# Softplus sums of a selective scan on GpSimd, its rounding on ScalarE, and the first chunk's gates projected behind its first step sizes

## Chip, cores and metric

One core of one Trainium2 chip runs the whole kernel. The metric is the device time of one execution in microseconds (us), as the median of several runs. The engines are TensorE (PE, matrix products into PSUM), VectorE (DVE), ScalarE (ACT, activation functions), GpSimd (POOL, SBUF only) and SyncE (SP, which only issues DMAs here). Each works through its own queue in order; they meet at semaphores.

## What is computed

A decoder layer over 2048 tokens of 256 features: a Mamba block with a feed-forward net, a cross attention over 1601 tokens, and a soft mixture of experts. The change touches the Mamba block alone:

```python
def mamba_block(x, ...):
    xz = x @ in_proj_w.T
    u, z = jnp.split(xz, 2, axis=-1)
    u = jax.nn.silu(causal_dwconv(u, conv_w, conv_b))
    x_dbl = u @ x_proj_w.T
    dt = x_dbl[..., :DT_RANK]
    ...
    delta = jax.nn.softplus(dt @ dt_proj_w.T + dt_proj_b)
    A = -jnp.exp(A_log)
    y = selective_scan(u, delta, A, Bm, Cm) + u * D
    y = y * jax.nn.silu(z)
    return y @ out_proj_w.T
```

The scan runs over time for each of 512 channels and 16 states: `h = exp(delta*A)*h + (delta*u)*B`, and `y` is the sum of `h*C` over the states.

## The kernel before

The tokens are cut into four chunks (`c`) of 512. In a chunk the 512 channels stand as four blocks of 128 partitions; two blocks are a half (`p` = 0 or 1), which is why most of the operands here are 128x1024. A chunk has 32 slots (`i`, `NU`), one for each half and state: slots 0 to 15 scan the first half, 16 to 31 the second. Over all chunks a slot is numbered `w` (0 to 127).

In a slot, ACT makes the decays `exp(delta*A)` of both blocks into PSUM (`decays`, L567), POOL makes `delta*u*B` for both (`scan_input`, L431, into a ring of three), DVE scans each block (L864), multiplies by C (`times_c`, L875) and keeps the last column (L882), and PE adds the products up in PSUM with a unit matrix (`add_states`, L1317). For one pair of slots in four POOL adds the two first (`add_pair`, L437), and PE waits for that. POOL may start the input of slot w when the scans of slot w-3 are done; ACT the decays of slot w when the products of slot w-2 are. B and C come by DMA on SP's queue, each two states ahead.

All else is laid by hand between these, by the number of the slot: each engine has one loop over chunks and slots with `if i == ...`. ACT's loop stands one slot ahead: at `i` it first makes the decays of slot i+1. Besides the scan of chunk c the loops carry the input side of chunk c+1 (transposing, in-projection, convolution `convolution` L812 and L816 at slots 9 to 12, gates `gate_input` L529, x_proj, step sizes) and the output side of chunk c-1 (`first_norm`, hidden blocks with Gelu at slots 23 to 30, `ffn_out`; `second_residual` L911, `second_norm` L921 and `mamba_out` L926 come in slots 2, 6 and 7 of the chunk after that).

The softplus is written as `relu(x) + log(1+e) + (e - ((1+e) - 1))` with `e = exp(-|x|)`. ACT makes |x| and relu (`step_input`, L544, L545), e (`step_exp`, L550) and the logarithm (`step_log`, L555); DVE the rounding `(1+e)-1` in one instruction of two operations (`step_rounded`, L826), the rest `e - ...` (`step_rest`, L831), the sum with the logarithm (`step_sum`, L837), and the addition to the relu (`step_size`, L844). `step_channels` (L852) is `delta*u`. Each is one instruction over a half, and happens eight times: for the first half of chunk 0 before the loop, for the second half of each chunk at slots 6 to 9, and for the first half of the next chunk at slots 24 to 28:

```python
if i == 6:
    step_rounded(c, 1)
...
if i == 8:
    step_sum(c, 1)
    step_size(c, 1)
if i == 9:
    step_channels(c, 1)
```

Before the loop, the first chunk is brought to its first step sizes: in-projection of the channels, then of the gates, convolution, Silus, x_proj (L1285), step sizes.

## Time and profile before

| | |
|---|---|
| median of 3 runs | 1638.02 us (1636.45 to 1638.27) |
| profiled execution, first to last instruction | 1636.5 us |
| scan of the Mamba block (first and last scan) | 49.7 to 660.7 us |
| busy over the span: PE, DVE, ACT, POOL | 1336.6, 797.4, 904.6, 402.9 us |
| busy from 100 to 200 us: PE, DVE, ACT, POOL | 63.4, 99.3, 48.4, 61.5 us |
| granted TensorE clock, mean | 0.90; 0.71 from 50 to 100 us, 0.78 from 100 to 200 us |

The profile was made on one execution; the times stand for that one. The page of the profile says of the granted TensorE clock what share of 2.4 GHz it is: 1.0 or 0.5 (1.2 GHz) at any moment. A float32 product shows as several passes of one instruction; "x8" in a row is their count. In the timeline, neighbouring instructions of one line are merged into one row, and a bracket names the idle time of the engine before it and what ended it.

### The profile page before, as it was taken

The numbers are of one execution on the slowest core, as the hardware profiler recorded it, in microseconds if no ns is written. First come the engines' busy times: TensorE is split into PE (matmuls) and PEld (weight loads), VectorE is DVE, ScalarE is ACT, GpSimd is POOL, SyncE is SP. The second block draws the span as 40 slices with busy tenths as digits, with TensorE's granted clock in tenths as the row PEclk, the third lists the DMA queues.
The fourth block names the chain that finished last, engine by engine and source line by source line (L and its number), as shares of the span: only waits on it lengthen the run. The fifth ranks groups of instructions, "written<-read, shape, count | busy, mean of one in ns | idle before, by whom it ended". The sixth has DMA issues, their size and how long they took to land.

```text
span 1636.5 us, 15496 instructions
## 1 busy us (share of the span) xinstructions
PE 1336.6 (82%) x5511; PEld 628.7 (38%) x5511; DVE 797.4 (49%) x1213; ACT 904.6 (55%) x1164; POOL 402.9 (25%) x177
## 2 busy tenths in 40 slices
PE   6477566887598748896735999999999988979999
PEld 2122123343334324653521223223223234568887
DVE  3899989989998899216520002001011016461011
ACT  3536444654466436122435997998998944751310
POOL 0637655654455466015030000000000001000000
PEclk9588787999789878998756999999999988989999
DMA  5323332332243233102994000000000000011701
GB/s 184 118 78 129 129 115 86 122 116 77 82 138 116 77 128 116 45 8 49 102 112 39 1 1 1 1 1 0 0 0 0 0 0 1 1 52 35 325 14 39
DMA packets 35633, 107.96 MB, mean 66 GB/s; under 512 B 3650, under 2 KB 14146, under 8 KB 32915
## 3 DMA queue, kind: packets, MB, share of 16 engines
q1 hardware_dynamic: 35572, 107.19, 23.7%
q8 instruction: 34, 0.56, 0.1%
q14 instruction: 27, 0.22, 0.1%
HBM read 93.60 MB, written 2.36 MB: 59 GB/s over the span
## 4 chain that ended last, share of the span: by engine, by line
PE 47%; DVE 24%; ACT 13%; issue 8%; DMA 5%; SPq 1%; POOL 1%; DVEq 0%; ACTq 0%; POOLq 0%
DVE ps L864 13%; PE ps L1558 10%; PE ps L1543 9%; ACT arena L706 6%; PE ps L1362 4%; PE ps L1667 4%; DMA arena<-arena 4%; PE ps L1708 3%; PE ps L1317 3%; DVE arena L875 2%; PE ps L1685 2%; PE ps L1696 2%; PE ps L1248 2%; SPq L377 1%; PE ps L1588 1%
## 5 line engine op out<-in xcount | busy, mean ns | idle before, releaser
L706 ACT ACTIVATE arena<-ps,bound 128x1024 f32<-128x1024 f32 (+1 forms) x416 | 421.1, 1215 | 26.7 <-PE ps L1543 26.7
L431 POOL TENSOR_TENSOR arena<-arena 128x1024 f32<-128x1024 f32 x128 | 300.7, 2353 | 262.0 <-DVE ps L864 218.1
L864 DVE TENSOR_TENSOR_SCAN ps<-ps,arena 128x512 f32<-128x512 f32 x256 | 327.3, 1279 | 18.1 <-ACT ps L567 13.7
L1317 PE MATMUL ps<-arena,ident 128*128 128x512 f32 x452 | 245.1, 683 | 106.1 <-POOL arena L437 66.1
L567 ACT ACTIVATE ps<-arena 128x512 f32<-128x512 f32 x256 | 173.1, 689 | 269.1 <-DVE arena L882 175.5
L1543 PE MATMUL ps<-arena 97*128 (+3 forms) x832 | 218.9, 385 | 22.8 <-issue 20.7
L1558 PE MATMUL ps<-arena 128*32 128x512 f32 (+1 forms) x1664 | 222.8, 607 | 1.1 <-ACT arena L706 0.9
L1317 PEld LDWEIGHTS ps<-arena,ident 128*128 128x128 f32 x452 | 91.5, 214 | 243.3 <-issue 89.0
L1141 DVE COPY arena<-ps 128x512 f32<-128x512 f32 x16 | 11.1, 691 | 355.8 <-PE ps L1558 355.8
L419 POOL TENSOR_TENSOR rstd<-ve,mhalf 128x4 f32<-128x4 f32 (+3 forms) x18 | 23.5, 1308 | 625.0 <-DVE ve L1166 469.9
L875 DVE TENSOR_TENSOR arena<-ps,arena 128x512 f32<-128x512 f32 x256 | 171.4, 669 | 0.0
L1543 PEld LDWEIGHTS ps<-arena 97*128 97x128 bf16 (+1 forms) x832 | 67.5, 99 | 227.0 <-ACT arena L706 140.6
L1248 PE MATMUL ps<-ident,arena 128*128 128x128 f32 x392 | 58.7, 291 | 40.4 <-DVE arena L1051 13.7
L1248 PEld LDWEIGHTS ps<-ident,arena 128*128 128x128 f32 x392 | 45.1, 147 | 76.0 <-issue 57.5
L1362 PE MATMUL ps<-arena 128*128 128x256 f32 x256 | 62.5, 400 | 12.1 <-ACT arena L583 12.1
L1558 PEld LDWEIGHTS ps<-arena 128*32 128x32 f32 (+1 forms) x1664 | 32.9, 108 | 95.5 <-ACT arena L706 78.3
L1262 PE MATMUL ps<-arena 128*128 128x512 f32 x128 | 62.9, 639 | 4.1 <-DVE arena L895 2.4
L1353 PE MATMUL ps<-arena 128*128 128x512 f32 x128 | 59.9, 615 | 5.5 <-ACT arena L583 4.8
L1667 PE MATMUL ps<-arena 128*128 128x257 f32 x256 | 58.6, 393 | 2.5 <-ACT arena L752 2.5
L1362 PEld LDWEIGHTS ps<-arena 128*128 128x128 f32 x256 | 50.0, 199 | 26.8 <-ACT arena L583 15.4
L1632 PE MATMUL ps<-arena 128*128 128x512 f32 x128 | 59.6, 609 | 0.0
L1708 PE MATMUL ps<-arena 128*128 128x256 f32 x256 | 55.5, 379 | 0.0
(178 smaller groups left out, 1386.5 us busy)
## 6 DMA issues: line engine op xcount, KB each, us to landing
arena<-bc_scratch SPq DMA_DIRECT2D x128, 512.0 KB, 3.7
arena<-in_mw SPq DMA_DIRECT2D x16, 1024.0 KB, 8.7
arena<-arena SPq DMA_DIRECT2D x48, 128.0 KB, 14.8
arena<-arena SPq DMA_DIRECT2D x12, 400.2 KB, 16.4
arena<-in_w SPq DMA_DIRECT2D x2, 1024.0 KB
out<-xt SPq DMA_DIRECT2D x4, 512.0 KB, 2.9
xt<-in_x SPq DMA_DIRECT2D x1, 1536.0 KB
arena<-in_ctx SPq DMA_DIRECT2D x1, 1200.8 KB, 7.8
```

The lines of the kernel that those rows point to most:

```text
L431: pool.tensor_tensor(dbu[:, w % DR], du[:, DP * p:DP * p + DP], over(bg[:, w // BG % 2, n % BG], DP), ALU.mult).then_inc(S["dbu_ready"], 1)
L567: act.activation(decay_bank(w, x), delta[:, d], ACT.Exp, scale=neg_a[:, d, n:n + 1]).then_inc(S["da_ready"], 1)
L706: act.activation(flat(prob[0:n, v % 2, 2 * h:2 * h + 2]), ps[0:n, 2 * (r % 3):2 * (r % 3) + 2, :].rearrange("p a b -> p (a b)"), ACT.Exp, ...
L864: dve.tensor_tensor_scan(decay_bank(w, x), decay_bank(w, x), dbu[:, w % DR, x], carry[:, d, n:n + 1], ALU.mult, ALU.add).then_inc(S["scan_ ...
L875: dve.tensor_tensor(state(w)[:, x], decay_bank(w, x), cg[:, w // BG % 2, n % BG], ALU.mult).then_inc(S["hc_ready"], 1)
L1248: return pe.transpose(dst, src, ident[:, :])
L1317: last = mm(bank(x), ident[:, :], state(2 * j + s)[:, x], start=False, stop=(j % HP == HP - 1 and (j in SUMMED or s == 1)))
L1362: mm(acc, gate[:, f, tok(i)], w2[:, f], start=(f == 0), stop=False)
L1543: last = mm(ps[0:n, 2 * (r % 3) + x, :], kx[0:XR + 1, head, b * P:b * P + n], qx[0:XR + 1, head, c * C:c * C + C] if first else qx[0:XR + ...
L1558: last = mm(ps[2 * HD * x:2 * HD * x + 2 * HD, 6 + g % 2, :], vx[0:n, b, G * g + x, :], prob[0:n, v % 2, x], start=(b == 0), stop=(b == KB ...
L1667: last = mm(ps[:, 4 + x if x < 4 else x - 4, 0:DM + 1], lg[:, t, tok(x)], xn[:, t, :], start=(t == 0), stop=(t == TT - 1))
L1708: last = mm(ps[:, t % 8, 0:DM], cwt[:, x, tok(t)], eo[:, x], start=(x == 0), stop=(x == NE - 1))
```

## The change

1. `step_rounded` is gone. ACT makes `1+e` and then `(1+e)-1` with two Identity activations in `step_log`, the logarithm after them.
2. `step_rest`, `step_sum` and `step_size` go to POOL's queue: for the second half behind the inputs of slots 7, 9 and 11, for the first half of the next chunk behind those of 24, 25 and 26. Only the first half of chunk 0 stays on DVE.
3. `step_channels` stays on DVE, at slot 14 instead of 9, and at slot 29 instead of 28.
4. In the first chunk, gates are projected behind x_proj and the first step sizes; ACT takes their Silus in its slot 1.

```diff
@@ -448,11 +448,42 @@
...
+            def step_rest(c, p):
+                h = c * DP + p
+                pool.wait_ge(S["sp_act"], h * 6 + 5)
+                pool.tensor_tensor(flat(sp_cor), flat(sp_exp), flat(sp_cor), ALU.subtract).then_inc(S["sp_step"], 1)
+
+            def step_sum(c, p):
+                h = c * DP + p
+                pool.wait_ge(S["sp_act"], h * 6 + 6)
+                pool.wait_ge(S["sp_step"], h * 2 + 1)
+                pool.tensor_tensor(flat(sp_cor), flat(sp_cor), flat(sp_ln), ALU.add).then_inc(S["sp_step"], 1)
+
+            def step_size(c, p):
+                h = c * DP + p
+                half = flat(delta[:, DP * p:DP * p + DP])
+                pool.wait_ge(S["sp_in"], h * DP + DP)
+                pool.wait_ge(S["sp_step"], h * 2 + 2)
+                pool.tensor_tensor(half, half, flat(sp_cor), ALU.add).then_inc(S["delta_ready"], 1)
+
             layer_norm_root(0)
             for c in range(NC):
+                more = c + 1 < NC
                 for i in range(NU):
                     w = c * NU + i
                     scan_input(w)
+                    if i == 7:
+                        step_rest(c, 1)
+                    if i == 9:
+                        step_sum(c, 1)
+                    if i == 11:
+                        step_size(c, 1)
+                    if i == 24 and more:
+                        step_rest(c + 1, 0)
+                    if i == 25 and more:
+                        step_sum(c + 1, 0)
+                    if i == 26 and more:
+                        step_size(c + 1, 0)
                     if w % 2 == 0 and w // 2 - 2 in SUMMED:
                         add_pair(w // 2 - 2)
...
 
             def step_exp(c, p):
                 h = c * DP + p
-                act.wait_ge(S["sp_act"], h * 4 + 2)
+                act.wait_ge(S["sp_act"], h * 6 + 2)
                 act.activation(flat(sp_exp), flat(sp_exp), ACT.Exp, scale=-1.0).then_inc(S["sp_act"], 1)
 
             def step_log(c, p):
                 h = c * DP + p
-                act.wait_ge(S["sp_act"], h * 4 + 3)
-                act.activation(flat(sp_ln), flat(sp_exp), ACT.Ln, bias=1.0).then_inc(S["sp_act"], 1)
+                act.wait_ge(S["sp_act"], h * 6 + 3)
+                act.activation(flat(sp_ln), flat(sp_exp), ACT.Identity, bias=1.0).then_inc(S["sp_act"], 1)
+                act.wait_ge(S["sp_act"], h * 6 + 4)
+                act.activation(flat(sp_cor), flat(sp_ln), ACT.Identity, bias=-1.0).then_inc(S["sp_act"], 1)
+                act.activation(flat(sp_ln), flat(sp_ln), ACT.Ln).then_inc(S["sp_act"], 1)
...
             for d in range(DB):
                 conv_input(0, d)
             for d in range(DB):
-                gate_input(0, d)
-            for d in range(DB):
                 channel(0, d)
             rank_b_c(0)
             step_input(0, 0)
@@ -606,6 +638,9 @@
                 for i in range(NU):
                     if c * NU + i + 1 < NW_ALL:
                         decays(c * NU + i + 1)
+                    if i == 1 and c == 0:
+                        for d in range(DB):
+                            gate_input(0, d)
                     if i == 3 and c >= 2:
                         second_squares(c - 2)
...
-            def step_rounded(c, p):
-                h = c * DP + p
-                dve.wait_ge(S["sp_act"], h * 4 + 3)
-                dve.tensor_scalar(flat(sp_cor), flat(sp_exp), 1.0, 1.0, ALU.add, ALU.subtract).then_inc(S["sp_step"], 1)
-
...
-                if i == 6:
-                    step_rounded(c, 1)
-                    if c >= 2:
-                        second_norm(c - 2)
-                if i == 7:
-                    step_rest(c, 1)
-                    if c >= 2:
-                        mamba_out(c - 2)
-                if i == 8:
-                    step_sum(c, 1)
-                    step_size(c, 1)
-                if i == 9:
+                if i == 6 and c >= 2:
+                    second_norm(c - 2)
+                if i == 7 and c >= 2:
+                    mamba_out(c - 2)
+                if i == 14:
                     step_channels(c, 1)
                 if i in (9, 10, 11, 12) and more:
                     convolution(c + 1, i - 9)
...
-                if more:
-                    if i == 24:
-                        step_rounded(c + 1, 0)
-                    if i == 25:
-                        step_rest(c + 1, 0)
-                    if i == 26:
-                        step_sum(c + 1, 0)
-                    if i == 27:
-                        step_size(c + 1, 0)
-                    if i == 28:
-                        step_channels(c + 1, 0)
+                if i == 29 and more:
+                    step_channels(c + 1, 0)
...
             conv_keep(0)
-            step_rounded(0, 0)
             step_rest(0, 0)
             step_sum(0, 0)
             step_size(0, 0)
...
             def gates(c, d):
                 if d < 2:
-                    pe.wait_ge(S["u_raw"], c * DB + DP + d + 1)
+                    if c:
+                        pe.wait_ge(S["u_raw"], c * DB + DP + d + 1)
+                    else:
+                        pe.wait_ge(S["sp_in"], d + 1)
                     if c >= 2:
                         pe.wait_ge(S["hsum_ready"], (c - 2) * 2 + d + 1)
                 else:
...
             pe.wait_ge(S["w_first"], 16 * 3)
             for d in range(DB):
                 channels(0, d)
+            rank_b_c(0)
+            step_input(0, 0)
             for d in range(DB):
                 gates(0, d)
-            rank_b_c(0)
-            step_input(0, 0)
             pe.wait_ge(S["w_mamba"], 16 * 6)
             pe.wait_ge(S["prep_dve"], 1 + DB)
```

**POOL's queue in chunk 0, from the input of slot 7 on.** L431 is `scan_input`, L437 `add_pair`; before:

```order
L431 TENSOR_TENSOR arena<-arena 128x1024 [waits scan_done]
L431 TENSOR_TENSOR arena<-arena 128x1024 [waits scan_done,b_even]
L437 TENSOR_TENSOR arena<-arena 128x1024 [waits hc_ready]
L431 TENSOR_TENSOR arena<-arena 128x1024 [waits scan_done]
L431 TENSOR_TENSOR arena<-arena 128x1024 [waits scan_done,b_odd]
L431 TENSOR_TENSOR arena<-arena 128x1024 [waits scan_done]
L431 TENSOR_TENSOR arena<-arena 128x1024 [waits scan_done,b_even]
```

and after, where L454 is `step_rest`, L460 `step_sum` and L467 `step_size`:

```order
L431 TENSOR_TENSOR arena<-arena 128x1024 [waits scan_done]
L454 TENSOR_TENSOR arena<-arena 128x1024 [waits sp_act]
L431 TENSOR_TENSOR arena<-arena 128x1024 [waits scan_done,b_even]
L437 TENSOR_TENSOR arena<-arena 128x1024 [waits hc_ready]
L431 TENSOR_TENSOR arena<-arena 128x1024 [waits scan_done]
L460 TENSOR_TENSOR arena<-arena 128x1024 [waits sp_step,sp_act]
L431 TENSOR_TENSOR arena<-arena 128x1024 [waits scan_done,b_odd]
L431 TENSOR_TENSOR arena<-arena 128x1024 [waits scan_done]
L467 TENSOR_TENSOR arena<-arena 128x1024 [waits sp_step,sp_in]
L431 TENSOR_TENSOR arena<-arena 128x1024 [waits scan_done,b_even]
```

Each of the three stands behind one input and ahead of the next; the pair of states (L437) is behind the rest.

**POOL's queue in chunk 0, from the input of slot 24 on**, before:

```order
L431 TENSOR_TENSOR arena<-arena 128x1024 [waits scan_done,b_even]
L437 TENSOR_TENSOR arena<-arena 128x1024 [waits hc_ready]
L431 TENSOR_TENSOR arena<-arena 128x1024 [waits scan_done]
L431 TENSOR_TENSOR arena<-arena 128x1024 [waits scan_done,b_odd]
L431 TENSOR_TENSOR arena<-arena 128x1024 [waits scan_done]
```

and after (the same lines):

```order
L431 TENSOR_TENSOR arena<-arena 128x1024 [waits scan_done,b_even]
L454 TENSOR_TENSOR arena<-arena 128x1024 [waits sp_act]
L437 TENSOR_TENSOR arena<-arena 128x1024 [waits hc_ready]
L431 TENSOR_TENSOR arena<-arena 128x1024 [waits scan_done]
L460 TENSOR_TENSOR arena<-arena 128x1024 [waits sp_step,sp_act]
L431 TENSOR_TENSOR arena<-arena 128x1024 [waits scan_done,b_odd]
L467 TENSOR_TENSOR arena<-arena 128x1024 [waits sp_step,sp_in]
L431 TENSOR_TENSOR arena<-arena 128x1024 [waits scan_done]
```

The rest, which waits for ACT, now stands between the input of slot 24 and the pair; sum and addition follow behind the next two inputs.

**ACT's queue ahead of the loop.** L517 copies the channels, L529 are the gates' Silus, L522 the channels' Silus, L535 the copy of x_proj's result; before:

```order
L517 ACTIVATE arena<-ps 128x512 [waits u_ps] x4
L529 ACT_TABLE_LOAD
L529 ACTIVATE arena<-ps 128x512 [waits z_ps] x4
L522 ACTIVATE arena<-arena 128x512 [waits conv_step] x4
L535 ACTIVATE arena<-ps 48x512 [waits xdbl_ps]
```

and after, where L548 is the copy, L553 the channels' Silus, L566 the copy of x_proj and L575 and L576 are |x| and relu:

```order
L548 ACTIVATE arena<-ps 128x512 [waits u_ps] x4
L553 ACT_TABLE_LOAD
L553 ACTIVATE arena<-arena 128x512 [waits conv_step] x4
L566 ACTIVATE arena<-ps 48x512 [waits xdbl_ps]
L575 ACTIVATE arena<-ps,chan 128x512 [waits dt_ps]
```

The gates' Silus no longer stand there.

**ACT's queue from the first exponential (L550) into slot 1.** Before (L555 is the logarithm, L567 the decays):

```order
L550 ACTIVATE arena<-arena 128x1024 [waits sp_act]
L555 ACT_TABLE_LOAD
L555 ACTIVATE arena<-arena 128x1024 [waits sp_act]
L567 ACT_TABLE_LOAD
L567 ACTIVATE ps<-arena 128x512 [waits delta_ready]
L567 ACTIVATE ps<-arena 128x512 x3
L567 ACTIVATE ps<-arena 128x512 [waits carry_done,hc_ready]
L567 ACTIVATE ps<-arena 128x512 [waits hc_ready]
L567 ACTIVATE ps<-arena 128x512 [waits carry_done,hc_ready]
L567 ACTIVATE ps<-arena 128x512 [waits hc_ready]
```

and after (L586 and L588 Identity, L589 the logarithm, L601 the decays, L560 the gates' Silus):

```order
L586 ACTIVATE arena<-arena 128x1024 [waits sp_act]
L588 ACTIVATE arena<-arena 128x1024 [waits sp_act]
L589 ACT_TABLE_LOAD
L589 ACTIVATE arena<-arena 128x1024
L601 ACT_TABLE_LOAD
L601 ACTIVATE ps<-arena 128x512 [waits delta_ready]
L601 ACTIVATE ps<-arena 128x512 x3
L601 ACTIVATE ps<-arena 128x512 [waits carry_done,hc_ready]
L601 ACTIVATE ps<-arena 128x512 [waits hc_ready]
L560 ACT_TABLE_LOAD
L560 ACTIVATE arena<-ps 128x512 [waits z_ps] x4
L601 ACT_TABLE_LOAD [waits carry_done]
```

Two Identity activations stand ahead of the logarithm's table, and the four Silus with their table, and one more for the decays, between the decays of slots 2 and 3.

## Rows read from the trace of the kernel before

**Rows 1.** Waits of DVE, 40 to 700 us: who <- whom: total us, times, longest.

```profile
DVE arena L911 <- PE ps L1364: 38.2, 5, 11.3
```

**Rows 2.** Groups by line, DVE and POOL, 0 to 900 us (columns as the page's part 5).

```profile
L864 DVE TENSOR_TENSOR_SCAN ps<-ps,arena 128x512 f32<-128x512 f32 x256 | 327.3, 1279 | 18.1 <-ACT ps L567 13.7 <-POOL arena L431 4.1
...
L831 DVE TENSOR_TENSOR arena<-arena 128x1024 f32<-128x1024 f32 x8 | 10.4, 1294 | 0.0
...
L837 DVE TENSOR_TENSOR arena<-arena 128x1024 f32<-128x1024 f32 x8 | 9.8, 1225 | 0.4 <-ACT arena L555 0.4
L844 DVE TENSOR_TENSOR arena<-arena 128x1024 f32<-128x1024 f32 x8 | 9.8, 1219 | 0.5
...
L826 DVE TENSOR_SCALAR arena<-arena 128x1024 f32<-128x1024 f32 x8 | 5.5, 693 | 12.0 <-ACT arena L550 12.0
...
L431 POOL TENSOR_TENSOR arena<-arena 128x1024 f32<-128x1024 f32 x128 | 300.7, 2353 | 262.0 <-DVE ps L864 218.1 <-DVE arena L852 37.8 <-DMA arena<-bc_scratch 6.0
```

**Rows 3.** Timeline, 0 to 75 us (start us, us, engine line op out<-in xcount [idle before]).

```profile
26.48 2.33 DVE L816 SCALAR_TENSOR_TENSOR arena<-arena,chan 128x512 f32<-128x512 f32 x3
...
30.00 2.17 ACT L522 ACTIVATE arena<-arena 128x512 f32<-128x512 f32 x4
...
34.41 0.59 ACT L535 ACTIVATE arena<-ps 48x512 f32<-48x512 f32 x1 [2.23 <-PE ps L1285]
```

**Rows 4.** Timeline, the same window, slots 1 to 3 of the first chunk.

```profile
54.65 0.69 ACT L567 ACTIVATE ps<-arena 128x512 f32<-128x512 f32 x1 [1.03 <-DVE arena L875]
...
61.60 3.78 PE L1300 MATMUL ps<-arena 16*128 16x512 f32 x4
...
63.48 1.29 DVE L864 TENSOR_TENSOR_SCAN ps<-ps,arena 128x512 f32<-128x512 f32 x1 [1.60 <-POOL arena L431]
```

**Rows 5.** Timeline, chunk 0, slots 23 to 28: DVE and ACT.

```profile
160.64 1.28 DVE L864 TENSOR_TENSOR_SCAN ps<-ps,arena 128x512 f32<-128x512 f32 x1
...
163.16 1.04 ACT L550 ACTIVATE arena<-arena 128x1024 f32<-128x1024 f32 x1
...
164.22 1.28 ACT L555 ACT_TABLE_LOAD   x1
...
164.26 1.28 DVE L864 TENSOR_TENSOR_SCAN ps<-ps,arena 128x512 f32<-128x512 f32 x1
...
165.52 1.06 ACT L555 ACTIVATE arena<-arena 128x1024 f32<-128x1024 f32 x1
...
166.04 0.71 DVE L826 TENSOR_SCALAR arena<-arena 128x1024 f32<-128x1024 f32 x1
...
184.77 1.22 DVE L852 TENSOR_TENSOR arena<-arena 128x1024 f32<-128x1024 f32 x1
```

**Rows 6.** Timeline, chunk 1, slots 23 to 30: PE, ACT and DVE.

```profile
313.35 1.98 PE L1317 MATMUL ps<-arena,ident 128*128 128x512 f32 x4 [1.85 <-POOL arena L437]
315.17 3.60 PE L1353 MATMUL ps<-arena 128*128 128x512 f32 x8
...
315.15 1.04 ACT L550 ACTIVATE arena<-arena 128x1024 f32<-128x1024 f32 x1
...
337.19 1.23 DVE L852 TENSOR_TENSOR arena<-arena 128x1024 f32<-128x1024 f32 x1
...
349.03 5.41 PE L1362 MATMUL ps<-arena 128*128 128x256 f32 x16 [5.28 <-ACT arena L583]
```

**Rows 7.** Timeline, chunk 1, slots 6 and 7: ACT and DVE.

```profile
224.31 1.06 ACT L550 ACTIVATE arena<-arena 128x1024 f32<-128x1024 f32 x1
...
229.88 1.29 DVE L864 TENSOR_TENSOR_SCAN ps<-ps,arena 128x512 f32<-128x512 f32 x1 [1.64 <-ACT ps L567]
```

**Rows 8.** Timeline, chunk 2, slot 6: DVE and POOL.

```profile
388.33 0.68 DVE L826 TENSOR_SCALAR arena<-arena 128x1024 f32<-128x1024 f32 x1
...
388.49 2.72 POOL L437 TENSOR_TENSOR arena<-arena 128x1024 f32<-128x1024 f32 x1 [1.66 <-DVE arena L875]
388.93 3.76 DVE L921 SCALAR_TENSOR_TENSOR arena<-arena,rstd,scales 128x256 f32<-128x256 f32 x4
```

More of the change, by code:

```diff
@@ L834, in step_sum @@
                 h = c * DP + p
-                dve.wait_ge(S["sp_act"], h * 4 + 4)
-                dve.wait_ge(S["sp_step"], h * 3 + 2)
+                dve.wait_ge(S["sp_act"], h * 6 + 6)
+                dve.wait_ge(S["sp_step"], h * 2 + 1)
                 dve.tensor_tensor(flat(sp_cor), flat(sp_cor), flat(sp_ln), ALU.add).then_inc(S["sp_step"], 1)
@@ L1281, in rank_b_c @@
             def rank_b_c(c):
-                pe.wait_ge(S["z_ready"], c * DB + 3)
+                if c:
+                    pe.wait_ge(S["z_ready"], c * DB + 3)
                 for d in range(DB):
@@ L1291, in step_input @@
                     pe.wait_ge(S["xdbl_ready"], c + 1)
-                    pe.wait_ge(S["z_ready"], c * DB + DB)
+                    if c:
+                        pe.wait_ge(S["z_ready"], c * DB + DB)
                     if c >= 2:
@@ L1296, in step_input @@
                     pe.wait_ge(S["sp_in"], c * DB + DP)
+                    if c == 0:
+                        pe.wait_ge(S["z_ready"], DB)
                     if c >= 2:
```

4 lines of the change are left out of this document (2 added, 2 removed).

## Prediction

> **What bounds the kernel now.** I read the waits of VectorE (DVE) first. Between 40 and 700 us, the stretch of the Mamba scan, its residual adds wait 38.2 us for TensorE (PE) [rows 1], and its scans 13.7 us for ScalarE (ACT) and 4.1 for GpSimd (POOL) [rows 2]; nearly everything else is DVE at work. So DVE sets the pace of the scan, one slot after another: a slot without extra work is 3.62 us long (160.64 to 164.26), and what follows the first scan and multiply of a slot starts 1.78 us behind the slot [rows 5]. An instruction taken from DVE is then worth its duration, as long as POOL has the next scan's input, and ACT its decays, in time. The question is whether they still have. The second view is therefore the timeline around the places where a half of the step sizes is made: seven times inside the loop, four times at slots 5 to 9 (the second half of a chunk) and three times at slots 23 to 28 (the first half of the next).
>
> **What leaves DVE.** Seven times a rounding (0.69), a rest (1.29), a sum (1.23) and an addition (1.22) [rows 2]: 4.43 each, 31 us in all. POOL pays 2.35 us for an instruction of the same shape [rows 2], so it gets 7 x 7.05 = 49 us. ACT gets two Identity passes in the place of the rounding; they aren't in the trace, and I take the 1.05 us of its exponential over the same 128x1024 elements [rows 5]; they cost more than nothing and there is no reason for more than 1.3. Seven times 2.1 is 15 us. Both engines have the room on average. What counts is the order on POOL's queue.
>
> **The first half of the next chunk, three times.** POOL runs ahead of DVE: it makes the input of slot w once scan w-3 is over. Behind the input of slot 24 it now meets the rest, which waits for ACT, and everything queued behind it waits too: the pair of states (the same shape, so 2.35) and the input of slot 25. In chunk 0 the exponential ends at 164.20 [rows 5]. Two Identity passes: 166.3. Rest, pair and input, 3 x 2.35: 173.35, and only then can scan 25 start (it could at 167.9). Then sum and input 26: 178.05, addition and input 27: 182.75; a slot lasts 3.62, so POOL sets both. Slot 28 starts at 182.75 + 3.62 = 186.4. Before it was 184.77 - 1.78 = 183.0 [rows 5]. So this place loses **3.4 us** where it should win 4.4.
>
> In chunk 1 the pair matters as well: PE stands before it (PE waits 1.85 us for it at 313.35, [rows 6]) with the feed-forward's matmuls behind it, and ACT's Gelu waits for those in front of the decays of slot 26. Exponential done 316.19 [rows 6], Identity 318.3, rest 320.65, pair 323.0 (before: 313.3). PE has been idle for over 10 us then; four passes at the lower clock take 3.8 us [rows 4], so 326.8; the eight passes of the first two hidden blocks take 3.6 at the full clock [rows 6], about 4 here: 330.8. Gelu 0.7 (as a decay of the same shape), table 1.28, decay 0.69 [rows 4, 5]: slot 26 starts at 333.5, slot 28 at 340.7. Before: 337.19 - 1.78 = 335.4 [rows 6]. **5.3 us** lost; if PE does not come into it, POOL's chain alone gives 338.4, or 3.0. Chunk 2 has the same order of work and a table of times that is within 0.4 us of this: 5.0. The three places: **+13.7 us** (9.4 to 14).
>
> **The second half, four times, without collisions.** Here ACT is one slot earlier against POOL, and the rest's wait does no harm. But ACT is on the path: in chunk 1 scan 7 waits 1.64 us for the decays that stand behind exponential, table, logarithm, table [rows 7]. With 2.1 more it starts at about 231.9 instead of 229.88. The three sums of 3.74 are gone behind it: -1.7. In chunk 0 the same shift, and sums that took 4.3 (one was held up): -2.3. In chunks 2 and 3 a norm (L921, 3.76 us) stands in the same slot and hides the shift: -3.7 each. Together **-11.4**.
>
> **The collisions.** Where the two engines read SBUF at once the trace shows that one holds the other up. POOL's pair wants to start at 388.49, while the rounding runs (388.33 to 389.01): it takes 2.72 instead of 2.35. The next DVE instruction, the norm's first, asks at 388.93, and is done only when POOL has finished at 391.2: four instructions that need under 2 take 3.76 [rows 8]. So POOL gets its turn between two DVE instructions, and DVE then waits for POOL's whole instruction. The scans and multiplies, whose states lie in PSUM, are not held up (256 scans, mean 1.28 [rows 2]). The Trainium skill's page "GPSIMD Engine Reference", section "Key points", names contention with DVE instructions of two SBUF inputs or in a two-port mode; by that rule, which speaks against this change, the trace agrees.
>
> Before, POOL's one input per slot ran beside PSUM work, and the convolution of the next chunk (slots 9 to 12; the last three of its four instructions take 2.33 us [rows 3], all SBUF) met an idle POOL. Now POOL is behind. Chunk 1: the exponential ends at 225.37 [rows 7], the rest starts at 227.5, and then follow without a gap input 8, pair, input 9, sum, input 10 (to 241.6), input 11, addition (to 246.3). DVE reaches the convolution at 231.9 + 2 x 3.62 + 1.78 = 240.9. The rest of input 10, all of input 11 and the addition go in between its four instructions: 0.7 + 2.35 + 2.35 = 5.4 us. Chunk 0 comes out the same (5.3), chunk 2 at 4.5; chunk 3 has no convolution. In chunks 2 and 3 the final addition of slot 7 waits 0.8 for the pair. Together **+17.0**. The bounds are nothing and this sum: between them the row with the turn taken decides.
>
> **The start.** The gates' Silus stood in front of those of the convolution. The convolution ends at 28.81, the first Silu started only at 30.00 and x_proj was read at 34.41 [rows 3]. Now the last Silu runs at once: 28.9 + 0.6 + two passes 0.9 = 30.4, a gain of 4.0 (1.8 if PE has fallen to the lower clock meanwhile). The logarithm is needed 2.1 later behind it: -1.9. In slot 1 ACT then has four Silus and two more tables: from 55.34 - 1.9 [rows 4] table 1.28 and two Silus 1.2, then PE's two blocks of four passes, 1.9 to 3.8 each [rows 4], Silu 0.6, table 1.28, decay 0.69: scan 3 between 63.6 and 65.5, against 63.48 [rows 4], where POOL's input made it wait 1.60. So the whole start comes to 0 to +2, or up to +4 with the low clock; **+1.0**. A rule on the two table loads: on the trace the load starts 0.02 us behind the exponential and the logarithm 0.02 behind the load [rows 5], 1.28 in all. The Trainium skill ("ScalarE: Activation LUTs", section "What ACT_TABLE_LOAD costs") puts a switch at some 2.66 us with its drain; by it the start would be 2.8 worse, as an estimate. I go by the row.
>
> **Sum.** 13.7 - 11.4 + 17.0 + 1.0 = +20.3 us. The profiled execution's span is 1636.5 us, inside the three runs (1636.45 to 1638.27); I add it to their median: 1638.0 + 20.3 = **1658.3 us**. Nothing behind the scan changes. PE's waits ahead of the residual adds don't swallow it: that chain starts from the last Gelu (PE waits 5.28 us for it at 349.03, [rows 6]), and this moves with the slots.
>
> **Rivals.**
> 1. DVE keeps the interface through a chain of its own instructions and waits once only, for the POOL instruction under way: about 5 us of the 17. +8.3, 1646.3. Against it: 388.93 [rows 8].
> 2. There are no collisions: +3.3, 1641.3. Against it the same row.
> 3. The cover holds, and the kernel is **faster**: POOL delivers the sums without making a scan wait. At slot 24 this needs the rest to start by 167.88 - 7.05 = 160.8; the exponential alone ends at 164.20 [rows 5]. Were it so, three times -4.4, with -11.4 and +1.0: -23.6, 1614.4. It could come about only if ACT reached the step's exponential some 5.5 us earlier against DVE; nothing in the change moves it.
> 4. The residual adds' waits on PE (38.2 us in all [rows 1]) do absorb what chunks 1 and 2 lose at slots 24 to 28: 10.3 less, 1648; with no collisions as well, -7.0 and 1631.0. Against it: the 5.28 us.
>
> The new order of the queues shows the sums on POOL in the places said, so that the change does what it says is not in doubt.
>
> **Chances.** A measurement of this kernel tells about 0.2% (3.3 us) from no change. Forecast 0.62 (its own range 1650 to 1667: the bounds of the second, third and last term). Rival 1: 0.16. Rival 2: 0.09, about half of it within 0.2%. Rival 3: 0.04. Rival 4: 0.09, with 0.02 on the fast side. So slower 0.86, same 0.08, faster 0.06. The range that should hold it 8 times in 10 takes in rival 1 and most of rival 4: 1643 to 1667.
>
> **What would show it.** Right: POOL waits for ACT once in slot 24 of chunks 0 to 2, and DVE's scans wait for POOL's input some 7 us at each such place, 20 us in all where it was 4.1; the convolution's instructions show single durations of 2.5 to 3 us; ACT shows two tables more. Wrong: convolution instructions all at 0.75 (rival 2), one long one a chunk (rival 1), or scans 25 to 27 that follow each other at 3.62 (rival 3). A residual wait on PE that shrinks by 5 in chunks 2 and 3 is rival 4.

## Result: 1.1% slower

| | changed kernel | before |
|---|---|---|
| median of 4 runs each | 1656.42 us (1652.61 to 1658.28) | 1637.24 us (1636.33 to 1638.27) |
| ratio, 95% interval | 1.0106 [1.0086, 1.0126] | |
| span of the profiled execution | 1655.1 us | 1636.5 us |
| predicted | 1658.3 us (1643 to 1667) | |

The page of the changed kernel, its totals and three of its groups (columns as in [rows 2]):

```profile
PE 1332.7 (81%) x5511; PEld 633.3 (38%) x5511; DVE 777.3 (47%) x1184; ACT 923.7 (56%) x1182; POOL 451.3 (27%) x198
...
L431 POOL TENSOR_TENSOR arena<-arena 128x1024 f32<-128x1024 f32 x128 | 302.1, 2368 | 190.3 <-DVE ps L894 138.3
L894 DVE TENSOR_TENSOR_SCAN ps<-ps,arena 128x512 f32<-128x512 f32 x256 | 327.3, 1279 | 56.3 <-ACT ps L601 34.9
L1337 PE MATMUL ps<-arena,ident 128*128 128x512 f32 x452 | 239.6, 677 | 132.8 <-POOL arena L437 124.5
```

DVE has 20 us of work less, of the 31 that were taken from it: the other 11 came back as longer instructions. POOL has 48 us more, ACT 19. The scans (L894, before L864) take what they took, 1.28 us, and wait 56.3 us instead of 18.1. Who they wait for stands in DVE's waits from 40 to 720 us (who <- whom: total us, times, longest):

```profile
DVE arena L941 <- PE ps L1384: 38.0, 6, 11.3
DVE ps L894 <- ACT ps L601: 34.9, 14, 5.3
DVE ps L894 <- POOL arena L431: 21.3, 6, 6.0
```

The residual adds (L941, before L911) wait for PE as before [rows 1]; the scans wait 21 us more for ACT and 17 more for POOL.

To see where the time comes in, I set the start of each of the 128 slots against the same slot of the kernel before. The last scan starts 20.5 us later, and 1.9 of that is given back behind the scan.

| place | predicted | later by |
|---|---|---|
| start, first scan | | 0.0 |
| start, scan 3, then slot 5 | +1.0 | +1.9, -1.2 |
| second half and convolution, chunk 0 | +3.0 | +2.0 |
| the same, chunk 1 | +3.7 | +3.6 |
| the same, chunk 2 | +1.6 | -0.8 |
| the same, chunk 3 (no convolution) | -2.9 | -2.8 |
| first half of the next, chunk 0 (slots 24 to 28) | +3.4 | +3.3 |
| the same, chunk 1 | +5.3 | +6.3 |
| the same, chunk 2 | +5.0 | +4.6 |

Smaller shifts elsewhere (-0.8 to +1.5 at a place) make the rest. The -0.8 of chunk 2 holds -1.7 at scan 6, ahead of any softplus work, which comes back in a kernel without the moved sums (see below, under what was left out). Chunk 0, slots 24 to 27, in the timeline of the changed kernel (columns as in [rows 3]):

```profile
168.02 1.06 ACT L586 ACTIVATE arena<-arena 128x1024 f32<-128x1024 f32 x1
169.11 1.06 ACT L588 ACTIVATE arena<-arena 128x1024 f32<-128x1024 f32 x1
...
170.24 2.35 POOL L454 TENSOR_TENSOR arena<-arena 128x1024 f32<-128x1024 f32 x1 [7.51 <-ACT arena L588]
172.55 2.34 POOL L437 TENSOR_TENSOR arena<-arena 128x1024 f32<-128x1024 f32 x1
174.85 2.34 POOL L431 TENSOR_TENSOR arena<-arena 128x1024 f32<-128x1024 f32 x1
177.16 2.34 POOL L460 TENSOR_TENSOR arena<-arena 128x1024 f32<-128x1024 f32 x1
177.23 1.29 DVE L894 TENSOR_TENSOR_SCAN ps<-ps,arena 128x512 f32<-128x512 f32 x1 [5.48 <-POOL arena L431]
...
181.84 1.29 DVE L894 TENSOR_TENSOR_SCAN ps<-ps,arena 128x512 f32<-128x512 f32 x1 [0.90 <-POOL arena L431]
...
186.47 1.29 DVE L894 TENSOR_TENSOR_SCAN ps<-ps,arena 128x512 f32<-128x512 f32 x1 [0.91 <-POOL arena L431]
```

POOL stands 7.5 us before the rest until ACT's second Identity is done. Rest, pair and input follow without a gap, and scan 25 waits 5.48 us for the last of them. In chunk 1 the pair is missed by PE too:

```profile
331.84 2.33 POOL L437 TENSOR_TENSOR arena<-arena 128x1024 f32<-128x1024 f32 x1
...
334.23 3.78 PE L1337 MATMUL ps<-arena,ident 128*128 128x512 f32 x4 [11.53 <-POOL arena L437]
...
336.51 1.29 DVE L894 TENSOR_TENSOR_SCAN ps<-ps,arena 128x512 f32<-128x512 f32 x1 [5.47 <-POOL arena L431]
...
337.81 4.88 PE L1373 MATMUL ps<-arena 128*128 128x512 f32 x8
...
341.01 0.69 ACT L617 ACTIVATE arena<-ps,chan 128x512 f32<-128x512 f32 x1 [5.27 <-PE ps L1373]
...
345.55 1.29 DVE L894 TENSOR_TENSOR_SCAN ps<-ps,arena 128x512 f32<-128x512 f32 x1 [5.32 <-ACT ps L601]
```

Pair, PE's adds, the hidden block (L1373), Gelu (L617), the decays behind it: scan 26 pays a second time, 5.32 us. This is what chunk 1 has over chunk 0. Before, PE waited 1.85 us for that pair [rows 6]; now it is 11.53.

The convolution of the next chunk at slot 9, in chunk 0, with slot 10 at the end for comparison, and then in chunk 1:

```profile
91.22 4.84 POOL L431 TENSOR_TENSOR arena<-arena 128x1024 f32<-128x1024 f32 x2
...
93.29 0.56 DVE L847 TENSOR_SCALAR arena<-arena,chan 128x512 f32<-128x512 f32 x1
93.88 6.26 DVE L851 SCALAR_TENSOR_TENSOR arena<-arena,chan 128x512 f32<-128x512 f32 x3
...
96.01 2.80 POOL L467 TENSOR_TENSOR arena<-arena 128x1024 f32<-128x1024 f32 x1
...
104.26 2.32 DVE L851 SCALAR_TENSOR_TENSOR arena<-arena,chan 128x512 f32<-128x512 f32 x3
```

```profile
246.89 4.65 POOL L431 TENSOR_TENSOR arena<-arena 128x1024 f32<-128x1024 f32 x2
...
249.63 2.20 DVE L847 TENSOR_SCALAR arena<-arena,chan 128x512 f32<-128x512 f32 x1 [0.72 <-ACT arena L548]
...
251.50 2.53 POOL L467 TENSOR_TENSOR arena<-arena 128x1024 f32<-128x1024 f32 x1
251.87 4.30 DVE L851 SCALAR_TENSOR_TENSOR arena<-arena,chan 128x512 f32<-128x512 f32 x3
```

The same three instructions take 6.26 and 4.30 us beside POOL, 2.32 without it: held up, +3.9 us in chunk 0 and +3.6 (with L847, 2.20 instead of 0.53) in chunks 1 and 2. The single instructions are either bare (0.75) or long: 2.73 and 2.72 in chunk 0, one of 2.72 in chunk 1.

### The profile page after: what moved, and what is told of

Its sections match the earlier page's. It is cut to its first block, busy times and chain, and to the rows that moved or that the text cites. A ratio compares the mean times of both kernels' runs of the same rounds, so it can differ in the third digit from the quotient of the medians.

```text
span 1655.1 us, 15505 instructions
## 1 busy us (share of the span) xinstructions
PE 1332.7 (81%) x5511; PEld 633.3 (38%) x5511; DVE 777.3 (47%) x1184; ACT 923.7 (56%) x1182; POOL 451.3 (27%) x198
## 4 chain that ended last, share of the span: by engine, by line
PE 46%; DVE 22%; ACT 13%; issue 8%; DMA 5%; POOL 3%; SPq 2%; DVEq 0%; ACTq 0%; POOLq 0%
DVE ps L894 11%; PE ps L1578 10%; PE ps L1563 9%; ACT arena L741 6%; PE ps L1382 4%; PE ps L1687 4%; DMA arena<-arena 3%; PE ps L1728 3%; PE ps L1337 3%; DVE arena L851 2%; PE ps L1705 2%; PE ps L1716 2%; POOL arena L431 1%; DVE arena L905 1%; PE ps L1261 1%
## 5 line engine op out<-in xcount | busy, mean ns | idle before, releaser
L431 POOL TENSOR_TENSOR arena<-arena 128x1024 f32<-128x1024 f32 x128 | 302.1, 2368 | 190.3 <-DVE ps L894 138.3
L894 DVE TENSOR_TENSOR_SCAN ps<-ps,arena 128x512 f32<-128x512 f32 x256 | 327.3, 1279 | 56.3 <-ACT ps L601 34.9
L1337 PE MATMUL ps<-arena,ident 128*128 128x512 f32 x452 | 239.6, 677 | 132.8 <-POOL arena L437 124.5
L601 ACT ACTIVATE ps<-arena 128x512 f32<-128x512 f32 x256 | 172.4, 689 | 242.0 <-DVE arena L912 151.2
L1261 PE MATMUL ps<-ident,arena 128*128 128x128 f32 x392 | 58.7, 291 | 39.9 <-DVE arena L1064 13.7
L1275 PE MATMUL ps<-arena 128*128 128x512 f32 x128 | 67.4, 674 | 18.5 <-ACT arena L560 16.1
L1382 PE MATMUL ps<-arena 128*128 128x256 f32 x256 | 62.3, 399 | 9.5 <-ACT arena L617 9.5
L1373 PE MATMUL ps<-arena 128*128 128x512 f32 x128 | 59.6, 614 | 0.7 <-ACT arena L612 0.7
L1652 PE MATMUL ps<-arena 128*128 128x512 f32 x128 | 59.6, 609 | 0.0
```

Of the source, the lines that this page charges most:

```text
L431: pool.tensor_tensor(dbu[:, w % DR], du[:, DP * p:DP * p + DP], over(bg[:, w // BG % 2, n % BG], DP), ALU.mult).then_inc(S["dbu_ready"], 1)
L601: act.activation(decay_bank(w, x), delta[:, d], ACT.Exp, scale=neg_a[:, d, n:n + 1]).then_inc(S["da_ready"], 1)
L894: dve.tensor_tensor_scan(decay_bank(w, x), decay_bank(w, x), dbu[:, w % DR, x], carry[:, d, n:n + 1], ALU.mult, ALU.add).then_inc(S["scan_ ...
L1261: return pe.transpose(dst, src, ident[:, :])
L1337: last = mm(bank(x), ident[:, :], state(2 * j + s)[:, x], start=False, stop=(j % HP == HP - 1 and (j in SUMMED or s == 1)))
L1382: mm(acc, gate[:, f, tok(i)], w2[:, f], start=(f == 0), stop=False)
```

## Experiments

The theory on trial is the prediction's: (a) POOL's queue, held by the rest that waits for ACT, starves the scans at slots 24 to 28, (b) POOL's late queue meets DVE's convolution and holds it, (c) ACT's two passes delay the decays. The rivals are that one of the three carries it all, or that the places where work stands (a late convolution, late sums) cost as such. Ratios are against the kernel before on the same chip, with their 95% intervals; "last scan" is its start against the kernel before.

### The two halves of the change

The gates alone, on the kernel before (the same three edits in ACT's and PE's order as in the diff, with the waits that they need):

```diff
                         decays(c * NU + i + 1)
+                    if i == 1 and c == 0:
+                        for d in range(DB):
+                            gate_input(0, d)
...
```

> The kernel before with part 4 of the change alone: the first chunk's gates behind its first step sizes; rounding and sums of the softplus stay on DVE. In the changed kernel the first scan starts when it did before (49.75 us) although two Identity passes of 2.1 us stand ahead of it, so the moved gates should bring 2.1 us up to there, and give back 1.9 at slot 3, where ACT has four Silus and two tables between the decays of slots 2 and 3. Theory: first scan at about 47.6 us, total -1.5 to 0 us against the kernel before. Rival (a table switch costs more than its 1.28 us row): slot 3 gives back 4 or more, total +2.

1635.88 us, ratio 0.999 [0.9981, 1.0], last scan -2.5. And the changed kernel without the moved gates (the reverse of that edit):

> The changed kernel without part 4: the gates of the first chunk stay ahead of x_proj. Theory: first scan 2.1 us later (51.8), the wait of slot 3 gone, total within 0 to +1.5 us of the changed kernel (1656.4), so +19 to +21 against before: what costs is in the sums and the rounding. Rival: the gates are part of the loss, total clearly below 1654.

1658.79 us, 1.0129 [1.0112, 1.0146], last scan +23.1. So the gates are worth some 2 us, and all of the loss is in the rest of the change. With the gates alone the first scan starts 3.7 us earlier (2.1 expected), and 2.4 of it is lost again at scan 3, which waits for ACT's four Silus in slot 1.

### ACT's rounding, and POOL's sums

The rounding on ACT, with the three sums on DVE at their old slots:

```diff
-                act.activation(flat(sp_ln), flat(sp_exp), ACT.Ln, bias=1.0).then_inc(S["sp_act"], 1)
+                act.activation(flat(sp_ln), flat(sp_exp), ACT.Identity, bias=1.0).then_inc(S["sp_act"], 1)
+                act.wait_ge(S["sp_act"], h * 6 + 4)
+                act.activation(flat(sp_cor), flat(sp_ln), ACT.Identity, bias=-1.0).then_inc(S["sp_act"], 1)
+                act.activation(flat(sp_ln), flat(sp_ln), ACT.Ln).then_inc(S["sp_act"], 1)
```

> The kernel before with the rounding alone moved to ACT (two Identity passes), the three sums still on DVE at their old slots, gates as before. Theory: ACT's chain exponential, (two passes), table, logarithm, table, decays is what scan 7 of chunks 0 and 1 and scan 25 of chunks 1 to 3 come to wait for: 2.1 us at the start, 2 us at each of two second halves and three first halves, nothing in chunks 2 and 3 at slot 7 where a norm hides it: +12 us, about 1649. Rival (ACT is busy 55% only, it has room; DVE saves 0.7 us seven times): -3 to 0 us.

1650.41 us, 1.0083 [1.0066, 1.0099], last scan +12.6. As expected: +2.1 at scan 7 of chunks 0 and 1, and about +2 at scan 25 of chunks 0 to 2 (expected at chunks 1 to 3). The two passes cost their 2.1 us wherever decays stand right behind them.

The sums on POOL, with the rounding left on DVE and the gates as before; against the changed kernel:

```diff
+                if i == 6:
+                    step_rounded(c, 1)
                 if i == 6 and c >= 2:
                     second_norm(c - 2)
...
```

> The three sums on POOL at the slots of the changed kernel, but the rounding stays on DVE at its old slots, gates as before. Theory: POOL's queue is held as long as before at slot 24 (the rounding ends at 166.75 against 166.3 for the second Identity), so the scans wait for POOL about 6 us there three times, and the convolutions collide as in the changed kernel; ACT's 2.1 us are missing from the start and from slots 6 and 7. +11 to +16 us against before, 1648 to 1653. Rival (ACT's passes are the cause of the loss): -10 us or more, since DVE loses 26 us of work.

1661.81 us, 1.015 [1.0133, 1.0166], last scan +23.7. That is a miss by 9 us, and 3 us worse than the same kernel with ACT's rounding (1658.79). Its timeline in chunk 2, slot 6:

```profile
403.01 0.68 DVE L857 TENSOR_SCALAR arena<-arena 128x1024 f32<-128x1024 f32 x1
403.61 7.94 DVE L952 SCALAR_TENSOR_TENSOR arena<-arena,rstd,scales 128x256 f32<-128x256 f32 x4
403.77 2.52 POOL L454 TENSOR_TENSOR arena<-arena 128x1024 f32<-128x1024 f32 x1 [2.88 <-DVE arena L857]
406.25 2.53 POOL L431 TENSOR_TENSOR arena<-arena 128x1024 f32<-128x1024 f32 x1
408.74 2.52 POOL L437 TENSOR_TENSOR arena<-arena 128x1024 f32<-128x1024 f32 x1
```

The rounding releases POOL's rest just as DVE begins its four norms. Norm and POOL instruction take turns, three times over: the first norm takes 0.48 us and the other three some 2.56 each, and the 3.76 us of the four [rows 8] become 7.94. This gives +4.2 in chunks 2 and 3, and chunk 0 loses 2.4 us more at its convolution than the changed kernel does. In the changed kernel ACT's passes hold the rest back until the norms are over: in chunk 2 there, the four end at 405.7 and the rest starts at 405.98, and no norm is held. So the parts don't add up (12.6, 23.7 and -2.5 make 33.8, the whole has 20.5): each sets when POOL's instructions fall.

### The order on POOL's queue

The pair ahead of the rest:

```diff
                     scan_input(w)
+                    if w % 2 == 0 and w // 2 - 2 in SUMMED:
+                        add_pair(w // 2 - 2)
                     if i == 7:
                         step_rest(c, 1)
...
-                    if w % 2 == 0 and w // 2 - 2 in SUMMED:
-                        add_pair(w // 2 - 2)
```

> The changed kernel with one exchange on POOL: at slots that have both, the pair of states goes ahead of the softplus step (slots 8k; it matters at slot 24, where the rest waits for ACT). Theory: the pair is made while POOL would wait, so scan 25 waits for POOL 3.1 us instead of 5.5 in chunks 0 to 2, and PE gets the pair as early as before, so the wait for ACT at scan 26 of chunks 1 and 2 (5.3 and 3.8) goes: -10 to -12 us against the changed kernel, 1645. Rival (PE and the pair have no part): -7 at most, by three times 2.35 us of queue; and scan 26 still waits for ACT in chunks 1 and 2.

1646.6 us, 1.0058 [1.0041, 1.0074], last scan +8.3. As expected (1645). Scan 25 is now late by about 2.5 in each chunk, and the second wait, at scan 26 of chunks 1 and 2, is gone:

```profile
170.30 2.36 POOL L454 TENSOR_TENSOR arena<-arena 128x1024 f32<-128x1024 f32 x1 [5.16 <-ACT arena L588]
...
172.62 2.34 POOL L431 TENSOR_TENSOR arena<-arena 128x1024 f32<-128x1024 f32 x1
...
175.00 1.29 DVE L894 TENSOR_TENSOR_SCAN ps<-ps,arena 128x512 f32<-128x512 f32 x1 [3.19 <-POOL arena L431]
```

The first halves' sums two slots later, behind the inputs of slots 26, 27 and 28:

```diff
-                    if i == 24 and more:
+                    if i == 26 and more:
                         step_rest(c + 1, 0)
...
-                if i == 29 and more:
+                if i == 30 and more:
                     step_channels(c + 1, 0)
```

> The changed kernel with the three sums of the first halves two slots later on POOL (behind the inputs of slots 26, 27, 28 instead of 24, 25, 26) and delta*u at slot 30 instead of 29; nothing else. Theory: the second Identity is done before POOL reaches the rest, so nothing is held: scans 25 to 27 of chunks 0 to 2 no longer wait for POOL, scan 25 waits some 2.7 us for ACT instead. Each of the three places goes from a loss of 3.4 to 6.3 us to a gain of up to 1.5: -15 to -17 us, 1640. Rival (POOL has too much to do there whatever the order): at most -5.

1639.85 us, 1.0013 [0.9996, 1.0029], last scan +5.0. Against the changed kernel this is the largest single gain, 16.6 us for four slot numbers. Scan 25 waits for ACT instead (2.89 at 175.70 in chunk 0, of which 2.1 are the two passes):

```profile
171.35 2.35 POOL L454 TENSOR_TENSOR arena<-arena 128x1024 f32<-128x1024 f32 x1
...
175.70 1.29 DVE L894 TENSOR_TENSOR_SCAN ps<-ps,arena 128x512 f32<-128x512 f32 x1 [2.89 <-ACT ps L601]
```

### Moving the convolution out of POOL's way

To slots 11, 12, 13, 14 in the changed kernel:

```diff
-                if i in (9, 10, 11, 12) and more:
-                    convolution(c + 1, i - 9)
+                if i in (11, 12, 13, 14) and more:
+                    convolution(c + 1, i - 11)
...
```

> The changed kernel with the four convolutions of the next chunk at slots 11 to 14 instead of 9 to 12 (and what follows them at 15), when POOL has worked off the sums of the second half. Theory: the collisions go, the convolution's instructions are back at 0.54 and 0.75 us: 4.0, 3.6 and 3.6 us in chunks 0 to 2, -11 us, 1645. Rival (the convolution was slow for its inputs, not for POOL): at most -1.

1651.55 us, 1.0083 [1.0067, 1.01], last scan +16.2: a miss, about 5 of the 11 us. The collision at slot 9 is gone, but in chunk 0 slot 14 has one:

```profile
120.66 1.22 DVE L882 TENSOR_TENSOR arena<-arena 128x1024 f32<-128x1024 f32 x1
...
121.95 2.58 POOL L431 TENSOR_TENSOR arena<-arena 128x1024 f32<-128x1024 f32 x1 [7.64 <-DVE arena L882]
122.37 6.25 DVE L851 SCALAR_TENSOR_TENSOR arena<-arena,chan 128x512 f32<-128x512 f32 x3
...
124.50 2.79 POOL L437 TENSOR_TENSOR arena<-arena 128x1024 f32<-128x1024 f32 x1
```

`delta*u` (L882) releases POOL's input of slot 16, a pair follows, and the convolution behind L882 walks into both. This is chunk 0 only. In chunks 1 and 2 POOL's input comes later (at 283.27 in chunk 1, behind the convolution), the convolution at slot 14 is bare, and the pair holds the small copy behind it (`conv_keep`, L856: 2.2 us instead of 0.17, at 285.73 in chunk 1). The first step at slot 11 is late by 1.0 to 1.4 in each chunk. Together the convolutions are held 7.7 us where it was 11.3, and the copies 4. The same with the first halves' sums late as well:

> The edits of the two experiments before together (sums of the first halves at 26 to 28, convolutions at 11 to 14), ACT rounding and moved gates as in the changed kernel. Theory: the two add up, -26 to -28 against the changed kernel: 1629, faster than before by 0.4 to 0.6%. Rival: one of them only moves the wait to ACT and they do not add: 1636 or more.

1636.37 us, 1.0001 [0.9985, 1.0017], last scan +0.4. A miss by 7 us, for the same reason: 7.6 us held in the convolutions, 4 in the copies. Then the fourth convolution at slot 15:

```diff
-                if i in (11, 12, 13, 14) and more:
-                    convolution(c + 1, i - 11)
+                if i in (11, 12, 13, 15) and more:
+                    convolution(c + 1, (11, 12, 13, 15).index(i))
...
```

> As the kernel with both later (first-half sums behind POOL's inputs 26, 27, 28; the convolutions of the next chunk at slots 11 to 14), but with the fourth convolution at slot 15 instead of 14. In the trace of the kernel with the convolutions at 11 to 14, the one at slot 14 took 6.25 us for its three steps instead of 2.33, because POOL, released by the product delta*u ahead of it (L882 at 120.66), made its input 16 and a residual pair over it (121.95 to 127.29). My theory (a DVE instruction on SBUF waits for POOL's running instruction, wherever it stands in the chunk): the fourth convolution at slot 15 meets an idle POOL, and 3.9 us go in each of three chunks, so 1636.4 - 12 = 1624.5 us. Rival (what costs is the convolution's place late in the chunk, since ScalarE's Silus of the next chunk and its gates wait for it, and with them the decays): slot 15 is then no better than slot 14, 1636 us or more, with new waits of the scans for ScalarE at slots 15 to 18.

1636.96 us, 0.9998 [0.9989, 1.0008], last scan +3.1. Nothing gained. The number is the rival's, but its sign is missing: DVE's waits for ACT are those of the kernel with the late sums (40.6 us in 18 waits, 38.4 in 18 there). The timeline says what happened:

```profile
124.80 2.35 POOL L437 TENSOR_TENSOR arena<-arena 128x1024 f32<-128x1024 f32 x1
...
125.96 1.48 DVE L847 TENSOR_SCALAR arena<-arena,chan 128x512 f32<-128x512 f32 x1
...
127.11 2.54 POOL L431 TENSOR_TENSOR arena<-arena 128x1024 f32<-128x1024 f32 x1
127.47 4.29 DVE L851 SCALAR_TENSOR_TENSOR arena<-arena,chan 128x512 f32<-128x512 f32 x3
```

I had made two mistakes. The 3.9 us that I had read in chunk 0 stood in chunk 0 alone. And I had taken POOL's idle time from the other run: with no convolution holding DVE at slot 14, scan and input 17 came earlier too, and POOL was busy here. The convolution at slot 15 is held 2.9, 3.9 and 3.9 us in the three chunks, so the four are held 14.7 us in all where it was 7.6; the copies, 4 us before, are bare. That is some 3 us more, and the last scan comes 2.7 later. The place has to be one at which POOL can't have work: behind the scans of its slot, with another convolution, since nothing new is released to POOL without a scan. Two at slot 12 and two at slot 13, in the changed kernel:

```diff
-                if i in (9, 10, 11, 12) and more:
-                    convolution(c + 1, i - 9)
+                if i in (12, 13) and more:
+                    for d in range(2 * i - 24, 2 * i - 22):
+                        convolution(c + 1, d)
...
```

> The changed kernel with the four convolutions of the next chunk moved from slots 9, 10, 11, 12 to slots 12, 12, 13, 13 (two in a slot), and nothing else. POOL has made up its queue by slot 12 (its inputs 13 and 14 end at 101.6 in the kernels with later convolutions), and it starts an input only when a scan has ended, so during the second convolution of a slot, which has no scan ahead of it, it stays idle; and all four stand ahead of delta*u of slot 14. My theory (held instructions alone): no convolution is held, the sums of 48 steps go from 44.0 us to 36.1 and the first steps from 12.0 to 8.6, so 11 us less than the changed kernel: 1645.5 us. Rival (the convolution's lateness or the loss of slack for ScalarE costs as much as the collisions, as the kernel with convolutions at 11 to 14 could also be read): 1651 us or more, with waits of the scans for ScalarE at slots 13 to 17 in place of the held instructions.

1645.14 us, 1.0043 [1.0023, 1.0063], last scan +9.5: the 11 us, with this edit alone. In its timeline POOL is idle from 104.1 to 110.84 and the convolutions take their bare time; in all three chunks they are held 0.2 us together, where the changed kernel has 11.3:

```profile
104.41 2.33 DVE L851 SCALAR_TENSOR_TENSOR arena<-arena,chan 128x512 f32<-128x512 f32 x3
...
107.23 2.33 DVE L851 SCALAR_TENSOR_TENSOR arena<-arena,chan 128x512 f32<-128x512 f32 x3
...
110.84 2.35 POOL L431 TENSOR_TENSOR arena<-arena 128x1024 f32<-128x1024 f32 x1 [6.75 <-DVE ps L894]
```

This settles (b): what cost was the company, not the convolution's place.

### A version that beats both

The changed kernel with the rounding back on DVE (at slot 6 behind the norm, and at slot 24), first halves' sums late, gates moved, convolutions at 11, 12, 13, 15:

```diff
+                if i == 6:
+                    step_rounded(c, 1)
...
+                if i == 24 and more:
+                    step_rounded(c + 1, 0)
...
```

> The kernel with the convolutions at slots 11, 12, 13 and 15 and the first-half sums late, with the rounding back on DVE (at slot 6 behind the norm of chunk c-2, and at slot 24), so that ScalarE makes only exp and Ln again. My theory: ScalarE's two extra passes cost what the kernel with the rounding alone showed (+2.1 at scans 7 and 25 by the wait for the decays, 12.6 us in all), and DVE's rounding costs 0.68 us times 7; so about 8 us less than the run beside it: 1616.5 us, with DVE's waits for ScalarE before scan 25 gone. Rival (DVE is what bounds, and POOL's rest right behind the rounding holds DVE as in the kernel with the sums alone on POOL): the 2.1 us come back as held instructions at slots 7 and 25, and it equals the run beside it or is slower, 1625 to 1635.

1626.14 us, 0.993 [0.9914, 0.9947], last scan -9.3, 10.8 less than with ACT's rounding beside it (8 expected; the 1616.5 of the expectation also counted on the gain that slot 15 didn't bring). The scans wait 23.3 us for ACT where it was 40.6. Then with the convolutions at 12, 12, 13, 13:

> The kernel with the rounding on DVE and first-half sums late (1626.1 us with its convolutions at 11, 12, 13, 15), now with the convolutions at 12, 12, 13, 13. In that run's trace the convolution at slot 11 began with 1.47 us instead of 0.54 and the one at slot 15 took 1.48 and 4.29 us instead of 0.54 and 2.33, beside POOL's inputs. Held instructions alone: 3.8 us less in each of three chunks, 1614.7 us. Rival (two convolutions in one slot, 5.8 us, keep the scans from ScalarE's, PE's and POOL's work of the following slots): 1626 us, with new waits at slots 13 to 15.

**1619.71 us, 0.9891 [0.9854, 0.9929]**, last scan -19.6. I expected 1614.7, 11.4 less than the run before. At the last scan it is 10.3 less, and in the medians 6.4. The difference is scatter between executions: the profiled ones, in which the last scans were compared, took 1628.61 and 1618.48 us, 10.1 apart. The first was the slowest of its four, the second is 1.2 under its median. DVE's waits in this kernel, 40 to 720 us:

```profile
DVE ps L896 <- ACT ps L598: 23.7, 15, 4.8
...
DVE ps L896 <- POOL arena L431: 2.5, 1, 2.5
```

POOL makes the scans wait once, at the start. So moving the sums pays, once the rounding, the rest of the first halves and the convolutions stand elsewhere. That the gain comes from the sums and not from the new place of the convolutions is argued, not measured: no run has the sums on DVE with the convolutions at 12 and 13. But in the kernel before no convolution was held, and its gates alone brought 2 us.

## Why the prediction was right

The time was 1.9 us below the forecast, the rise in the span 18.6 where 20.3 was predicted. By its own steps:

- **First halves, +13.7 predicted, +14.2 measured.** The chain ACT, rest, pair, input, scan 25 stands in the rows above, and so does the way by PE and Gelu in chunk 1. The two runs on POOL's order show both: without the pair behind the rest the second wait goes, with the rest two slots later the first. The wait of the scans for POOL was given as 20 us and is 21.3.
- **Second halves, -11.4.** Chunk 3, which has no convolution, shows the term alone: -2.8 where -3.7 and a collision of 0.8 made -2.9. The price of the two Identity passes, taken from the exponential's 1.05 us, is 1.06.
- **Collisions, +17.0 predicted, about +12.3 measured** (3.9, 3.6 and 3.6 at the convolution, 0.6 twice at the last addition, L956). The mechanism is right, the size over a quarter too large. (The term's own parts, 5.3, 5.4, 4.5 and twice 0.8, make 16.8.) The step that was mis-sized is "The rest of input 10, all of input 11 and the addition go in between its four instructions". In chunk 1 the convolution waited 0.72 us for ACT's copy (L548) and began at 249.63, when input 10 was over (249.23) and input 11 under way: two POOL instructions held it, not three. And of a hold only the part behind the DVE instruction's request counts: L847 paid 1.67 for input 11 and the first L851 1.97 for the addition, 3.6 where 5.4 was put. The kernel with the convolutions at 12 and 13 measures the term by taking it away: 11.3 us.
- **The start, +1.0.** By the last row below, the first scan started as it had (49.75 instead of 49.73), for the lower bound that was named: PE had fallen to the lower clock (0.50 granted from 31 to 35 us), and four passes took 3.77 us instead of 1.98. This differs from execution to execution. The kernel with the convolutions at 11 to 14 has the same start; there the clock in these 4 us was 1.00, the passes took 1.98 and the first scan came at 48.28. Scan 3 comes +1.9. Of the four steps of the norm in slot 4 (L800) one was held up before, 1.63 us instead of 0.40, and none is now, which I hadn't counted: -1.2. Together +0.7. The prediction's bounds for scan 3, 63.6 to 65.5, don't follow from the durations that it names: these add up to 62.3 to 66.1. The measured 65.33 lies in both.

```profile
31.41 3.77 PE L1320 MATMUL ps<-arena 16*128 16x512 f32 x4 [0.68 <-ACT arena L566]
...
41.05 1.28 ACT L589 ACT_TABLE_LOAD   x1
...
49.75 1.29 DVE L894 TENSOR_TENSOR_SCAN ps<-ps,arena 128x512 f32<-128x512 f32 x1 [2.51 <-POOL arena L431]
```

- **Left out**: shifts that come to +3.6 in places with no edit nearby (+1.2 in slots 17 to 21 of chunk 0, +1.5 each at slots 3 and 22 of chunk 3, and small ones of either sign), and 1.9 given back behind the scan, where I had said that nothing changes. In chunk 0, half of the +1.2 is one more held step (L835, 0.98 us instead of 0.41, at slot 20). Those of chunk 3 (+1.5 twice) are not shown to come from the sums: the kernel with the gates alone has +1.7 and +1.5 at the same slots, and it has the -1.7 at scan 6 of chunk 2 too. Their cause wasn't tried.
- **The sum.** Against the forecast of +20.3 the first halves came +0.5, the second halves with their collisions -3.6 (+2.0 by the table instead of 5.6), the start -0.3, the other places +3.6 and the end -1.9. That makes 18.6. The mechanisms were right; that the total is closer than its parts is luck.
- **The rivals.** Rival 1 (DVE waits once only) fails on 93.88, which spans two POOL instructions; rival 2 on the same row. Rival 3, the cover that holds, isn't this kernel; but the last run comes near what it described, with the rest later instead of ACT earlier. Rival 4 (the residual adds' waits absorb it) fails: they are 38.0 us where they were 38.2 [rows 1]. The signs that were named for the forecast are there: waits for POOL of 21.3 us in all, convolution instructions of 2.73 and 2.72 us, and two table loads more on ACT (57 instead of 55 up to 900 us).

The table loads follow the row that the prediction went by: Identity ends at 41.04, the load starts at 41.05 and the logarithm at 42.34. The Trainium skill's drain ("ScalarE: Activation LUTs", section "What ACT_TABLE_LOAD costs") doesn't show here either.

## What to carry to other kernels

An instruction that is moved to a queue takes its wait along, and everything behind it in that queue inherits the wait: ask for each what is the latest place that still meets its deadline, and put it there, behind the work that others need. On DVE and GpSimd, add up not only how busy each is but what each does at the same moment; at each turn an instruction with its data in SBUF can cost DVE up to GpSimd's whole instruction (2.35 us here), whatever its own length. A free moment read from one trace may be gone once the edit is made: choose a place where the other engine can't have been released. And look at every place where the pattern should repeat, not at the first one: the collision at slot 14 stood in one chunk of three.

## What the runs showed of the hardware

- DVE and GpSimd take turns on SBUF, instruction by instruction, though DVE's queue was ready all the time: four norms of 128x256 took 3.76 us beside one POOL instruction [rows 8] and 7.94 beside three. POOL's own 2.35 grew to 2.52 to 2.80 in the rows above, and to 3.34 at most in the changed kernel (at 412.89, over an addition of 1.82). The Trainium skill ("SBUF — State Buffer", section "Who interferes with whom") calls the port pair that the two share an exclusive lock, and says, of DVE's two-port modes, that whoever issues first has it for the whole instruction while the other is fully blocked. The trace agrees, and for instructions with two operands in SBUF as well: the convolution step that began at 93.88 beside an input that ran to 96.06 ended at 96.61, 0.55 behind it.
- It holds for instructions with one SBUF tensor too: L847, a multiply and add with scalars, took 2.20 instead of 0.53. The scans and the multiplies, with one operand in PSUM, kept 1.28 and 0.67 beside POOL throughout (256 of each, at most 1.29 and 0.68).
